# Selective-scan recurrence: three of sixteen products B·dt·u as scaled copies of the turned layout, B and C rows in float32, products with C in pairs of states

## The reference, cut to what matters

```python
def step(h, inp):
    dt_t, B_t, C_t, u_t = inp
    dA = jnp.exp(dt_t[..., None] * A)
    h = dA * h + (dt_t * u_t)[..., None] * B_t[:, None, :]
    return (h, jnp.einsum('bdn,bn->bd', h, C_t))
_, ys = jax.lax.scan(step, h0, ...)
y = ys.transpose(1, 0, 2) + u * D_skip
return y * jax.nn.silu(z) @ W_out.T
```

## Time and profile before

| what | value |
|---|---|
| runs | 756.58, 759.32, 759.8 us; median 759.32 |
| profiled execution, its own time | 756.54 us |
| its span (first to last instruction) | 754.4 us |
| mean granted TensorE clock | 0.941 |
| the recurrence in it | 42.5 to 470.5 us |

### The profile page before, as it was taken

How to read it: one execution, slowest core, us unless ns; L and a number is a source line. 1 busy time by engine, 2 the same in 40 slices (tenths; PEclk the granted TensorE clock), 3 DMA queues, 4 the chain that set the end, 5 groups by cost and what they waited for, 6 DMA issues and landing times.

```text
span 754.4 us, 10800 instructions
## 1 busy us (share of the span) xinstructions
PE 599.6 (79%) x3563; PEld 253.5 (34%) x3591; DVE 570.3 (76%) x589; ACT 440.6 (58%) x662; POOL 473.5 (63%) x254
## 2 busy tenths in 40 slices
PE   4866786787887777967868787978986969999994
PEld 2311121221221112312212222446663335777751
DVE  4498998998998999999989998445562435666643
ACT  3977577578578567676685752444544224555521
POOL 6379999999999999999999999500003200000002
PEclk9998798899998998998989999999999889999997
DMA  3499576576576676775775662000001110000001
GB/s 98 103 290 316 196 252 233 215 244 237 199 257 200 235 257 217 234 237 199 251 238 202 255 227 87 1 1 2 2 11 46 45 44 1 2 1 2 1 1 60
DMA packets 34009, 107.48 MB, mean 142 GB/s; under 512 B 7061, under 2 KB 7582, under 8 KB 33950
## 3 DMA queue, kind: packets, MB, share of 16 engines
q1 hardware_dynamic: 31382, 102.89, 40.7%
q10 hardware_dynamic: 1928, 2.65, 1.1%
q0 software_dynamic: 640, 1.18, 0.5%
HBM read 98.84 MB, written 4.19 MB: 137 GB/s over the span
## 4 chain that ended last, share of the span: by engine, by line
PE 40%; issue 17%; DVE 16%; POOL 15%; ACT 6%; DMA 3%; SPq 1%; DVEq 0%; POOLq 0%; ACTq 0%
POOL hc L1763 8%; POOL dbu L1774 7%; DVE hh_all L1463 6%; PE py L229 6%; PE pb L198 6%; PE px L252 5%; PE py L714 5%; DVE pb L1458 4%; PE pb L925 2%; PE px L741 2%; DMA cc<-scr 2%; PE pb L702 1%; PE px L242 1%; PE py L949 1%; DVE yg L1472 1%
## 5 line engine op out<-in xcount | busy, mean ns | idle before, releaser
L1763 POOL TENSOR_TENSOR hc<-hh_all,cc 128x1024 f32<-128x1024 f32 x128 | 298.0, 2347 | 2.3 <-DVE hh_all L1463 1.3
L714 PE MATMUL py<-hc,w_cst 64*64 64x512 f32 x1024 | 153.3, 658 | 26.9 <-POOL hc L1763 17.1
L1463 DVE TENSOR_TENSOR_SCAN hh_all<-da,pb 128x1024 f32<-128x1024 f32 x72 | 164.6, 2286 | 2.5
L1777 POOL TENSOR_TENSOR yg<-w_xs 128x512 f32<-128x512 f32 x10 | 12.7, 1266 | 239.3 <-DVE w_xs L1599 153.0
L1463 DVE TENSOR_TENSOR_SCAN hh_all<-pb,dbu 128x1024 f32<-128x1024 f32 x56 | 127.7, 2280 | 17.5 <-POOL dbu L1774 14.1
L1774 POOL TENSOR_TENSOR dbu<-bb,dtu_all 128x1024 f32<-128x1024 f32 x56 | 131.5, 2349 | 0.0
L702 PE MATMUL pb<-bc,w_sel 128*128 128x512 bf16 x118 | 41.8, 421 | 71.6 <-DVE hh_all L1463 67.6
L1169 ACT ACTIVATE pb<-dt_all,w_aneg 128x1024 f32<-128x1024 f32 x56 | 62.6, 1118 | 58.3 <-DVE hh_all L1463 56.7
L1458 DVE TENSOR_TENSOR pb<-pb,dtu_all 128x1024 f32<-128x1024 f32 x72 | 87.5, 1215 | 1.8 <-DVE dtu_all L1444 0.2
L285 DVE TENSOR_REDUCE gate_all<-pb 128x1 f32<-128x1024 f32 (+7 forms) x64 | 60.4, 985 | 29.6 <-PE pb L208 14.8
L1169 ACT ACTIVATE da<-dt_all,w_aneg 128x1024 f32<-128x1024 f32 x72 | 80.5, 1137 | 0.5
(11 more groups left out here) (292 smaller groups left out, 951.2 us busy)
## 6 DMA issues: line engine op xcount, KB each, us to landing
cc<-scr SPq DMA_DIRECT2D x128, 512.0 KB, 4.4
bb<-scr SPq DMA_DIRECT2D x56, 512.0 KB, 4.7
out<-yg ACTq DMA_DIRECT2D x8, 256.0 KB, 2.5
w_xs<-hc SPq DMA_DIRECT2D x6, 256.0 KB, 4.5
w_xst<-in_x SPq DMA_DIRECT2D x2, 512.0 KB, 5.3
scr<-bcf SPq DMA_DIRECT2D x8, 128.0 KB, 3.7
w_xs<-dt_all SPq DMA_DIRECT2D x4, 256.0 KB, 5.6
w_xs<-dtu_all SPq DMA_DIRECT2D x4, 256.0 KB, 5.9
```

Of the source, the lines that this page charges most:

```text
L714: last = nc.tensor.matmul(py[part(t), half(r)], ident[part(r), part(r)], hc[u % NHC][part(r), half(t)], start=(n == 0), stop=(n == NS - 1) ...
L1463: nc.vector.tensor_tensor_scan(hh[u % NHH][:, :], decay[:, :], drive[:, :], 0.0, ALU.mult, ALU.add).then_inc(scan_done, 1)
L1763: nc.gpsimd.tensor_tensor(hc[u % NHC][:, :], hh[u % NHH][:, :], cc[u % NCC][:, :], ALU.mult).then_inc(hc_done, 1)
```

## The change

- Pooled states fall from 7 to 6 of 16. Three more states are "crossed": 5, 10, 15, or in the sequences 0, 1, 3 and 5 ("shifted", whose other pieces come one unit later too) 6, 11, 15. Seven are left as own units.
- A crossed unit's drive: per sequence TensorE turns `dtu` in eight 128x128 blocks (`pe_dtu_t`), ScalarE copies it out (`act_dtu_t`); TensorE turns the rows of B in four blocks (`pe_b_t`), ScalarE copies the needed columns to `b_t` (`act_b_t`). With time on partitions, B_n is one number per partition: ScalarE makes eight scaled copies of 128x128 (`act_cross`), TensorE turns them back into `pb[u % 2]` (`pe_cross`), and VectorE scans from there with no product of its own.
- The rows of B and C stay in float32: one copy per half (`act_bc`) replaces the three-part split; the copies are the source of the DRAM scratch too, now in two DMAs. `pe_b` becomes a float32 matmul for each half of time, one over partitions 0 to 63 and one over 64 to 127.
- `pool_hc` takes two units in one instruction of 2048 elements (units 2 to 125; the first and last two stay single), with `hc` in four buffers, and LAG = 4. Scans, sums and loads of `cc` that wait for it now wait for a pair (`hc_count`).
- The output projection moves to n = 15, its copies to n = 0 of the next sequence; some pieces of the next sequence move by one or two units. Without the bf16 parts `sel`, two matrices and several copies at the start go.

```diff
-        POOLED = (1, 4, 6, 8, 10, 12, 14)
-        NHH, NHC, NCC, NDA, NDB, LAG = 4, 3, 4, 3, 2, 3
+        POOLED, CROSSED = ((1, 3, 6, 8, 11, 13), (1, 3, 5, 8, 10, 13)), ((5, 10, 15), (6, 11, 15))
+        NHH, NHC, NCC, NDA, NDB, LAG = 4, 4, 4, 3, 2, 4
+        def shifted(q):
+            return 1 if q == 0 or (q % 2 and q < LAST) else 0
+        def cross_step(u):
+            return u - (3 if u % NS == NS - 1 and shifted(u // NS) else 2)
+        def hc_count(u):
+            if u < 2:
+                return u + 1
+            return 2 + u // 2 if u < UNITS - 2 else u + 3 - UNITS // 2
...
+        def pe_b_t(pe, s):
+            if s:
+                pe.wait_ge(px_free[1], freed(s) + 1)
+            else:
+                pe.wait_ge(bc_done, 2)
+            for j in range(4):
+                last = nc.tensor.transpose(b_turned_at(s)[:, block_at(j)], bcs[s % 2][:, block_at(j)], ident)
+            last.then_inc(b_turned, 1)
+        def pe_dtu_t(pe, s):
+            for h in range(2):
+                pe.wait_ge(px_free[h], freed(s) + 2 if s else 1)
+                for j in range(4):
+                    last = nc.tensor.transpose(px[h][:, block_at(j)], dtu[s % 2][:, block_at(4 * h + j)], ident)
+                last.then_inc(dtu_turned, 1)
+        def pe_cross(pe, u):
+            atleast(pe, scan_done, u - 1)
+            pe.wait_ge(cross_done, cross_count(u) + 1)
+            for j in range(8):
+                last = nc.tensor.transpose(pb[u % 2][:, block_at(j)], cross[:, block_at(j)], ident)
+            last.then_inc(cross_full, 1)
         def pe_b(pe, u):
             if u >= UNITS or pooled(u):
                 return
+            if crossed(u):
+                pe_cross(pe, u)
+                return
...
-                last = nc.tensor.matmul(pb[u % 2][:, half(h)], w["sel"][:, n, :], bc3[q % 2][:, half(h)], start=True, stop=True)
+                last = nc.tensor.matmul(pb[u % 2][:, half(h)], cst[part(h), SELV + n:SELV + n + 1].broadcast_to((C, 128)),
+                                        bcs[q % 2][part(h), :], start=True, stop=True)
...
-        def act_hi(act, s, h):
...
-        def act_mid(act, s, h):
...
-        def act_lo(act, s, h):
...
+        def act_bc(act, s, h):
...
+            nc.scalar.activation(bcs[s % 2][part(h), :], bc_at(s, h)[part(h), :], ACT.Copy).then_inc(bc_done, 1)
...
+        def act_cross(act, u):
+            q, n = divmod(u, NS)
+            act.wait_ge(b_t_done, q + 1)
+            act.wait_ge(dtu_t_done, 2 * q + 2)
+            atleast(act, cross_full, cross_count(u))
+            for j in range(8):
+                last = nc.scalar.activation(cross[:, block_at(j)], dtu_t[:, block_at(j)], ACT.Copy, scale=b_t[:, q % 2, 2 * (j % 4) + j // 4, n:n + 1])
+            last.then_inc(cross_done, 1)
...
+                for v in range(u + 2, u + 4):
+                    if v < UNITS and crossed(v) and cross_step(v) == u:
+                        act_cross(act, v)
...
-            atleast(dve, hc_done, u - NHH + 1)
+            atleast(dve, hc_done, hc_count(u - NHH))
...
-        def pool_hc(pool, u):
-            pool.wait_ge(scan_done, u + 1)
-            pool.wait_ge(c_in[u % NCC], 16 * (u // NCC + 1))
+        def pool_hc(pool, u, count):
+            pool.wait_ge(scan_done, u + count)
+            for v in range(u, u + count):
+                pool.wait_ge(c_in[v % NCC], 16 * (v // NCC + 1))
...
-            atleast(pool, hc_used, 2 * (u - NHC + 1))
-            nc.gpsimd.tensor_tensor(hc[u % NHC][:, :], hh[u % NHH][:, :], cc[u % NCC][:, :], ALU.mult).then_inc(hc_done, 1)
+            atleast(pool, hc_used, 2 * (u + count - NHC))
+            here = slice(u % NHC * L, (u % NHC + count) * L)
+            nc.gpsimd.tensor_tensor(hc_all[:, here], hh_all[:, here], cc_all[:, here], ALU.mult).then_inc(hc_done, 1)
...
-            for u in range(UNITS):
-                pool_drive(pool, u + 2)
-                pool_hc(pool, u)
+            for u in range(0, UNITS, 2):
+                if u in (0, UNITS - 2):
+                    for v in (u, u + 1):
+                        pool_drive(pool, v + 2)
+                        pool_hc(pool, v, 1)
+                else:
+                    for v in (u, u + 1):
+                        pool_drive(pool, v + 2)
+                    pool_hc(pool, u, 2)
```

More of the change, by code:

```diff
@@ L395, in build_all @@
         yg = [sb(f"yg_{i}", [DI, L]) for i in range(2)]
-        bc3 = [sb(f"bc3_{i}", [128, L], BF16) for i in range(2)]
-        bcf = sb("bcf", [32, L])
+        bcs = [sb(f"bcs_{i}", [128, HALF]) for i in range(2)]
         da = [sb(f"da_{i}", [DI, L]) for i in range(NDA)]
@@ L401, in build_all @@
         hh = [hh_all[:, i * L:(i + 1) * L] for i in range(NHH)]
-        hc = [sb(f"hc_{i}", [DI, L]) for i in range(NHC)]
-        cc = [sb(f"cc_{i}", [DI, L]) for i in range(NCC)]
+        hc_all, cc_all = sb("hc_all", [DI, NHC * L]), sb("cc_all", [DI, NCC * L])
+        hc = [hc_all[:, i * L:(i + 1) * L] for i in range(NHC)]
+        cc = [cc_all[:, i * L:(i + 1) * L] for i in range(NCC)]
         bb = [sb(f"bb_{i}", [DI, L]) for i in range(2 if NP else 0)]
@@ L692, in pe_gate, with b_turned_at @@
             last.then_inc(px_full[h], 1)
+        def b_turned_at(s):
+            return (px[1] if s else pb[1])[:, 0:HALF]
+        def pe_b_t(pe, s):
[18 more added lines that the diff above has]
+            last.then_inc(cross_full, 1)
         def pe_b(pe, u):
@@ L987, in _ @@
                 pe_var(pe, 1, h)
-            for h in range(2):
-                pe_bc_less_hi(pe, 0, h)
+            pe_b_t(pe, 0)
             for h in range(2):
                 pe_dt_add(pe, 0, h)
-            for h in range(2):
-                pe_bc_less_mid(pe, 0, h)
-            pe.wait_ge(sel_done, 5)
+            pe.wait_ge(sel_done, 1)
+            pe.wait_ge(sd_done, 4)
             pe_b(pe, 0)
@@ L1025, in _ @@
             pe_qk(pe, 0)
+            pe_sum(pe, UNITS - 4)
             pe_first_pair(pe, NS)
@@ L1163, in act_exp @@
             else:
-                k = own_count(u)
+                k = da_count(u)
                 if k >= NDA:
-                    behind = next(v for v in range(u - NDA, -1, -1) if not pooled(v) and own_count(v) == k - NDA)
+                    behind = next(v for v in range(u - NDA, -1, -1) if not pooled(v) and da_count(v) == k - NDA)
                     act.wait_ge(scan_done, behind + 1)
@@ L1169, in act_exp, with act_dtu_t, act_b_t @@
             nc.scalar.activation(to[:, :], dt[q % 2][:, :], ACT.Exp, scale=w["aneg"][:, n:n + 1]).then_inc(da_done, 1)
+        def act_dtu_t(act, s):
+            atleast(act, cross_done, cross_count(NS * s))
+            for h in range(2):
+                act.wait_ge(dtu_turned, 2 * s + h + 1)
+                nc.scalar.activation(dtu_t[:, half(h)], px[h][:, :], ACT.Copy).then_inc(dtu_t_done, 1)
+        def act_b_t(act, s):
+            act.wait_ge(b_turned, s + 1)
+            nc.scalar.activation(b_t[:, s % 2, :, :], b_turned_at(s).rearrange("p (j r) -> p j r", r=C)[:, :, 0:NS], ACT.Copy).then_inc(b_t_done, 1)
+        def act_cross(act, u):
[6 more added lines that the diff above has]
+            last.then_inc(cross_done, 1)
         def act_out(act, b, h):
@@ L1329, in _ @@
             act.preload_act_table_set("exp_and_others")
-            for piece in (act_dt, act_one, act_hi, act_ln):
+            for piece in (act_dt, act_one, act_bc, act_ln):
                 for h in range(2):
@@ L1685, in _ @@
             for h in range(2):
-                dve_copied(dve, bcf[:, half(h)], bc_at(0, h)[0:32, :], (hi_done, h + 1), bcf_done)
-            for h in range(2):
-                dve_copied(dve, bc3[0][64:128, half(h)], bc_at(0, h)[64:128, :], (bc0_full[h], 2), mid_done)
-            for h in range(2):
                 dve_zn(dve, 1, h)
-                dve_copied(dve, bc3[0][96:128, half(h)], bc_at(0, h)[96:128, :], (bc0_full[h], 3), lo_done)
             for h in range(2):
@@ L1922, in sp_scratch @@
                     sp.wait_ge(bb_in[i], 16 * ((NP * (s - 1) + 1 - i) // 2))
-            sp.dma_start(scr[s % 2, :, :], bcf[:, :]).then_inc(scr_in, 16)
+            for h in range(2):
+                sp.dma_start(scr[s % 2, :, half(h)], bcs[s % 2][C * h:C * h + 32, :]).then_inc(scr_in, 16)
         def sp_c(sp, u):
@@ L2039, in constants @@
     t[:, CAUS:CAUS + 128] = np.where(r[None, :] <= r[:, None], 0.0, -1e30)
-    for part in (0, 64, 96):
+    for part in (0, 64):
         t[part:part + 32, SELV:SELV + 32] = np.eye(32)
```

194 lines of the change are left out of this document (96 added, 98 removed).

## The result

The changed kernel takes 774.46 us (median of 4, 773.25 to 775.24) against 758.96 (median of 4, 756.58 to 759.80) on the same chip: a ratio of 1.0208, 95% interval 1.0181 to 1.0235. It is slower by 15.5 us, where 736 was forecast and 752 was the upper end of the range.

A forecast was written before the change was run, and what follows sets the result against it. GpSimd was taken to bound the recurrence: 756.5 - 18.5 (fewer products) - 9.5 (pairs) + 4.0 (idle) + 0.9 (start) = 733.4 us, 23.1 less; from the median 759.3 that gives 736 us, range 726 to 752.

The forecast's parts named there:

- the pairs: GpSimd's products with C: 62 instructions over 2048 elements replace 124, saving 0.153 us each, 9.5 us; bounds 0 and 25.
- I put 0.5 us of idle GpSimd per sequence: GpSimd's idle time from late transfers, low clock and the crossed chain: 4.0 us added in all, at most 20.
- need is near 44 of 49.7: TensorE's load per sequence: about 44 us of work needed within the 49.7 us that GpSimd takes.
- The end (sum, y, out) keeps its order: Closing sum, y and output pieces: order unchanged by the edit, so no time was added for them.
- It fits by 1.15. The others have more: Crossed unit's ScalarE and TensorE chain: 4.5 us against 5.65 available for unit 6 of a shifted sequence, more slack elsewhere.
- +0.9: Start of the recurrence: the cc load of unit 5, now needed with unit 4's, makes GpSimd wait 0.9 us more.
- GpSimd sets the pace: Recurrence: GpSimd's 184 products of 2.315 us, 426.0 us with 2.3 of waiting, fill the stretch from 42.53 to 470.54.
- (a): Rival: GpSimd idles 1.5 to 2.5 us per sequence through lockstep with VectorE, giving 744 to 752 us; chance 0.23.
- its ring: Product buffers shared by scans and pairs: one round takes 10.1 us against GpSimd's 11.3 or 13.6, so it doesn't bind.
- (c): Rival: crossed products come late at ScalarE's in-order queue, a 7.6 us chain, 47 us added, 783 us; chance 0.09.
- The first sign of being wrong: Recurrence: the prediction counts as wrong if a sequence takes over 51.5 us.
- the stretch behind the recurrence changes by more than 2 us: Attention, feed-forward and end of program: carried over unchanged; a change above 2 us counts as the prediction being wrong.

The follow-up runs named there:

- e12: Kernel before with only the output projection's twenty-four matmuls joined behind unit 15 and its copy behind unit 0 of the next sequence; 764.34 us, ratio 1.0075.
- e5: Changed kernel with the output projection split again, eight matmuls behind unit 14 and sixteen behind unit 15; 766.97 us, ratio 1.0095 to before.
- e8: Changed kernel without crossed units (seven pooled products) and with the output projection back behind units 13 and 14; 775.63 us, ratio 1.0194 to before.
- e6: Changed kernel with pooled unit 3 of the unshifted sequences at 4 again; 773.43 us, ratio 1.0169 to before.
- e10: e7 with one ScalarE copy of 1024 columns per crossed unit in place of eight of 128, so outputs differ; 758.88 us, ratio 0.9990 to before.
- e7: Changed kernel with the projection split behind units 14 and 15, pooled unit 4 in unshifted sequences and six product buffers; 763.62 us, ratio 1.0057 to before.
- e2: Changed kernel with the products with C one by one again instead of in pairs; 773.25 us, ratio 1.0185 to before.
- e3: Kernel before with the pairs alone (four product buffers, sums four units behind); 763.41 us, ratio 1.0068.
- e14: Kernel before with each B product in eight matmuls of 128 columns in place of two of 512; 763.99 us, ratio 1.0064.
- e17: e7 with two crossed units per sequence in place of three, plus 24 ScalarE copies that compute nothing of the output; 762.41 us, ratio 1.0027 to before.
- e18: e7 with two crossed units per sequence in place of three, plus 64 ScalarE copies that compute nothing of the output; 759.44 us, ratio 1.0030 to before.

## Why the prediction was wrong

**What held.** The work and nearly all prices. Products on GpSimd fell by 26.0 us against 28.0: the B·dt·u products by 18.2 (18.5), the pairs by 7.8 (9.5). A pair of 2048 elements takes 4.53 us; the Trainium skill (GPSIMD Engine Reference, Performance versus the Vector engine) has 4497 ns, and the trace agrees within 1%. The float32 B product takes 1.13 us as its nearest row said, eight turned blocks 1.06 (1.94 at the low clock), eight scaled copies 2.43 against 2.3; their mean of 0.387 lies above the plain copy's 0.286. VectorE's load per sequence was to be 47.9 and was 46.8 in 55, ScalarE's 42.7 and 41.5, TensorE's 47.2 and 48.6.

**What failed.** The stalls: "I put 0.5 us of idle GpSimd per sequence, 4.0 in all; bounds 0 and 2.5 each, 20". Measured are 38.8 us, of which 2.3 were there before: 36.5, in place of 4.0 and the 0.9 for the start, 1.8 times the upper bound. The sum went by loads ("need is near 44 of 49.7") and by the cycles through a pair and through a crossed unit; it never went through the order of TensorE's and ScalarE's queues. Five places in it failed:

- The projection has no term. It had moved from behind 13 and 14 to behind 15, right in front of x, gate and y; "The end (sum, y, out) keeps its order" can be meant only of the end of the recurrence. e12 puts 4.9 us on this edit (764.34 against 759.44) in the kernel before; in the changed one e5's median fell by 7.5 us, its profiled recurrence by 5.4; in the kernel without crossed units it is nothing (e8).
- The pooled unit moved from 4 to 3 has none either; its exp stands in front of the Silu (e6: 10.8 us less waiting for y, 1 us of median).
- "It fits by 1.15. The others have more", of the crossed unit's chain, looked for table loads ahead of the copies on ScalarE; at 240.63 the instructions for dt stand there: TensorE waits 24.1 us for the copies in all, up to 4.84 at a time, and e10 puts 5.9 us of recurrence on them.
- "+0.9" for `cc` of units 4 and 5 was the first pair's wait for DMA: GpSimd idles 4.81 us there (up to 66.09) against 1.00, and still 4.90 in e7. The two loads were issued from 56.12 to 58.65, behind the eight spreads.
- "GpSimd sets the pace" was carried over: once its work had fallen by 26 us, a chain through TensorE, ScalarE and VectorE was longer, so what more it saves is idle time (e2). Of the terms priced as gains, pairs alone lose 0.7% (e3).

**The rivals.** (a), "lockstep bites", had idle GpSimd and late B products right and stopped at less than half the size; its ring isn't what bound, since single products gain nothing (e2) and no wait of a scan for a product with C of 0.2 us or more shows among VectorE's waits. (c), the one that said slower, had 0.09, and had the crossed copies on ScalarE right as one cause. VectorE itself didn't wait for turned blocks; TensorE did for the copies, and passed it on. The first sign of being wrong came too: a sequence takes 55 us, over 51.5.

**What wasn't thought of.** The end of the program, 5.9 us. That "the stretch behind the recurrence changes by more than 2 us" was my own sign of being wrong, and it did: 6.1 us, 5.9 of them in the end, where e14, e17 and e18 move it without any change to the work.

**What adds up.** 774.5 less 10.8 (e7) is 763.6; less the 5.9 of the end it would be 757.7, within 1.3 us of the time of before. The 26 us of GpSimd work then still buy nothing: e7's GpSimd idles 27.5 us. Its ScalarE copies hold 5.9 of them (e10), and 4.9 are the one wait for `cc`, whose removal wasn't tried; the rest is open, and so is why the same move of the projection costs 4.9 us in one kernel and nothing in another.
